# Gate and up steps of a quantized feed-forward layer: the step-size chain spread to one operation a step, and the second half's gate product moved from VectorE to GpSimd

## The chip, the cores and the metric

The kernel runs on one core of a Trainium2 chip. The metric is the device time of one execution in microseconds; lower is better. TensorE (PE in the profile) multiplies matrices into PSUM, VectorE (DVE) and ScalarE (ACT) do elementwise work and read PSUM, GpSimd (POOL) does elementwise work on SBUF tensors, and the SyncE queue (SP) issues the DMAs. The engines run side by side and are held in order by semaphores.

## The reference, cut to what matters

Two layers follow one another. The change lies where the second layer's feed-forward block and the first part of its state-space mixer are computed together, both from the normalized x:

```python
# feed-forward block: int4 weights with one scale per group of 128 inputs
Wg, Wu, Wd = dequant(gate_q, gate_s), dequant(up_q, up_s), dequant(down_q, down_s)
inner = silu(x @ Wg.T) * (x @ Wu.T)          # 1792 channels = 14 tiles of 128
g = silu(inner @ Wd.T)
# mixer: the step size of each of 128 heads and its running sum in chunks of 128 tokens
dt = softplus(h @ w_dt.T + dt_bias)          # = max(v, 0) + log(1 + exp(-|v|))
A_cs = cumsum(-exp(A_log) * dt)              # inside each chunk
```

1024 tokens stand as two halves (n = 0, 1) of 512 columns; channels are on the 128 partitions.

## The kernel before, in words

`layer1_inputs` computes `inner` in KI = 14 steps, one tile m of 128 channels a step. A step has both halves, n = 0 and then n = 1. For each half there are four groups k of 128 inputs, and for each of them a gate part and an up part: TensorE multiplies the unscaled integer weights with the tokens (`pe_group`, two passes each, L1075 and L1076) into one of four PSUM banks. The scales come in on the way out: ScalarE copies groups 0 and 1 with their scale into two sums (`act_group`, L1128), VectorE adds groups 2 and 3 to them (`dve_groups`, L1280, four operations a half), GpSimd adds the two sums (`add_sums`, L1574, two operations a half), ScalarE takes the silu of the gate part (`act_silu`, L1137), and the product of gate and up is `inner` (`dve_inner`, L1292, on VectorE for both halves). For the first half `inner` is split at once into a high and a low part for TensorE (`act_in` L1154, `dve_in_lo` L1269) and multiplied with the down weights of the step before; the down weights are scaled by VectorE (`dve_scale_down`, L1297) and split by ScalarE (`act_down`, L1143) and GpSimd (`rest_down`, L1579). GpSimd also turns the next tile's integer weights to floats (`whole_gate_up`, L1568). For the second half `inner` stays in the SBUF tensor `inner1` until all 14 steps are over; then 14 down steps (i = 14 to 27) multiply it.

Into the same steps the step-size chain is laid: `act_size` (step 1), `act_exps` (end of step 1), `act_plus_one` (step 2), `dve_rest` (steps 2 and 3), `act_logs` (end of step 3), `dve_dt` (two operations in each of steps 4 and 5), `dve_sums` (one operation and four scans in each of steps 6 and 7). The running sums `acs` are stored to DRAM by SP in step 10.

Each engine runs its instructions in the order in which they are written. On VectorE a step m is: four `dve_groups` of half 0; the product of step m - 1, half 1; `dve_scale_down`; the chain's part; the product of step m, half 0; four `dve_groups` of half 1; `dve_in_lo`. On GpSimd it is: two `add_sums` of step m - 1, half 1; `whole_gate_up`; two `add_sums` of step m, half 0; `rest_down`. Tiles are named by their memory: `sum_a` of odd steps lies in m_group, of even steps in f_sum_a and m_wdt; `sum_b` is g_stage; `inner1` is f_inner.

Of the kernel before, what the change touches and what calls it, by code (L numbers as in the profile page):

```python
# [9 lines left out]
ALU = mybir.AluOpType  # L10
# [915 lines left out]
def layer1_inputs(nc, a, xn, mv, x1_stored, ident, ones, h_hi, h_lo, xn_hi, xn_lo, std, normw, gu_s, group_dram,  # L926
# [9 lines left out]
    with ExitStack() as ctx:  # L936
# [50 lines left out]
        def gated(m):  # L987
            return inner1[:, (4 if m < 6 else 12) + m % 2, :]

# [61 lines left out]
        def half_at(m, n): return 2 * m + n  # L1051
# [126 lines left out]

        def act_exps(act):
            for n in range(NB):  # L1180
                act.wait_ge(act_chain, n + 1)
                nc.scalar.activation(e[:, n, :], rest[:, n, :], ACT.Exp, scale=-1.0).then_inc(act_chain, 1)
            nc.scalar.activation(aexp[:], alog[:], ACT.Exp).then_inc(aexp_ready, 1)
# [5 lines left out]

        def act_logs(act):  # L1190
            for n in range(NB):
                act.wait_ge(rest_ready, n + 1)
                nc.scalar.activation(u1[:, n, :], u1[:, n, :], ACT.Ln).then_inc(ln_ready, 1)

# [21 lines left out]

        def dve_dt(link, n):

            dve, c = nc.vector, slice(n * SEQ, (n + 1) * SEQ)
            dve.wait_ge(rest_ready, n + 1)  # L1220
            link(dve.scalar_tensor_tensor(rest[:, n, :], v[:, n, :], 0.0, rest[:, n, :], ALU.max, ALU.subtract))
            dve.wait_ge(ln_ready, n + 1)
            dve.tensor_tensor(dt[:, c], rest[:, n, :], u1[:, n, :], ALU.add).then_inc(dt_ready, 1)

        def dve_sums(link, n):

            dve, c = nc.vector, slice(n * SEQ, (n + 1) * SEQ)
            step = e[:, n, :]
            dve.wait_ge(dt_ready, n + 1)
            dve.wait_ge(aexp_ready, 1)  # L1230
            link(dve.tensor_scalar(step, dt[:, c], aexp[:, 0:1], -1.0, ALU.mult, ALU.mult))
            dve.wait_ge(gu_f_ready, 1)
            for t in range(TB):
                at = slice((n * TB + t) * P, (n * TB + t + 1) * P)
                dve.tensor_tensor_scan(acs[:, at], ones[:], step[:, t * P:(t + 1) * P], 0.0, ALU.mult,
                                       ALU.add).then_inc(acs_ready, 1)
# [45 lines left out]

        def dve_inner(dve, m, n):
            dve.wait_ge(silu_ready[n], m + 1)
            dve.wait_ge(sum_ready, 2 * half_at(m, n) + 2)
            if n == 0 and m >= 2:
                dve.wait_ge(in_lo_ready, m - 1)
            if n == 0 and m < 2:
                dve.wait_ge(h_lo_ready[1], m + 1)
            if n == 1 and m in (4, 5, 12, 13):  # L1290
                dve.wait_ge(in_lo_ready, m + 1)
            nc.vector.tensor_tensor(gated(m) if n == 0 else inner1[:, m, :], sum_a(m, n, 0), sum_a(m, n, 1),  # L1292
                                    ALU.mult).then_inc(inner_ready[n], 1)

# [23 lines left out]
        def _(sp):  # L1318
# [17 lines left out]
            for m in range(KI):  # L1336
                if m >= 2:
                    load_gate_up(m)
                load_down(m)
                if m == KI - 4:  # L1340
                    sp.wait_ge(acs_ready, NT)
                    sp.dma_start(acs_dram, acs[:]).then_inc(stored, 16)
# [72 lines left out]
        def _(act):  # L1415
# [21 lines left out]
            for m in range(KI):  # L1437
                if m:
                    act_group(act, m, 0, 0)
                    act_group(act, m, 0, 1)  # L1440
                    act_silu(act, m - 1, 1)
                if m == 1:
# [18 lines left out]
                if m == 1:  # L1461
                    act_exps(act)
                if m == 3:
                    act_logs(act)
            for i in range(KI, 2 * KI):
# [33 lines left out]
        def _(dve):  # L1499
# [31 lines left out]
            for m in range(KI):  # L1531
                if m:
                    dve_groups(dve, m, 0)
                    dve_inner(dve, m - 1, 1)
                dve_scale_down(dve, m + 1)
                if m in (2, 3):
                    dve_rest(m - 2)
                if m in (4, 5):
                    dve_dt(link, m - 4)
                if m in (6, 7):  # L1540
                    dve_sums(link, m - 6)
                dve_inner(dve, m, 0)
                if m < KI - 1:
                    dve_groups(dve, m, 1)
                    dve_in_lo(dve, m)
# [3 lines left out]
            for i in range(KI, 2 * KI):  # L1549
                if i == KI:  # L1550
                    dve_in_lo(dve, i)
                if i + 1 < 2 * KI:
                    dve_scale_down(dve, i + 1)
                    dve_in_lo(dve, i + 1)
                if i == KI + 2:
                    dve_inner(dve, KI - 1, 1)
                if i in (TURN_AT - 1, TURN_AT):
# [5 lines left out]
        def _(pool):  # L1563
# [33 lines left out]
            for m in range(KI):  # L1597
                if m:
                    add_sums(m - 1, 1)
                    if m + 1 < KI:  # L1600
                        whole_gate_up(m + 1)
                add_sums(m, 0)
                rest_down(m)
            for i in range(KI, 2 * KI):
                rest_down(i)
                if i == KI:
                    add_sums(KI - 1, 1)
                if W_AT < i <= W_AT + 4:
                    c, half = divmod(i - W_AT - 1, 2)
# [1269 lines left out]
```

## Time and profile before

| | |
|---|---|
| time, median of 3 runs | 1969.28 us (1967.21 to 1970.44) |
| the profiled execution's own time | 1965.4 us |
| its span, first to last instruction | 1963.6 us |
| PE busy | 1925.8 us, 98% |
| DVE busy | 1559.5 us, 79% |
| ACT busy | 1551.9 us, 79% |
| POOL busy | 1384.2 us, 70% |
| granted TensorE clock, mean | 0.999 |

The span is what the instructions cover; the execution's own time is 1.8 us more. The 14 steps lie between about 203 and 360 us of the span, the 14 down steps behind them up to about 408 us. Matmuls are pipelined: the record of one lasts 0.39 us, but the next starts 0.23 us after it, so a stretch in which PE is never idle can still hold fewer matmuls than it could. What counts is how many of them it starts.

### The profile page before, as it was taken

Reading aid. Unit: us, or ns where it says so; the run is one execution under the profiler, and the core shown is the slowest. Engines: PE = TensorE matmul, PEld = TensorE weight load, DVE = VectorE, ACT = ScalarE, POOL = GpSimd, SP = SyncE. Lnnn points to the kernel's source line nnn. Section 1 sums busy time; section 2 is a strip of 40 time slices with the busy share of each in tenths; the row PEclk is TensorE's granted clock in tenths of the full one; section 3 lists DMA queues with packets and bytes.
Section 4 is the critical chain, followed back from the end, with each engine's and each line's share of the span. In section 5 each row is a group of like instructions: output and inputs, shape, how many; then the busy total and the mean of one; then the engine's idle time right before and its main releaser. Section 6 shows DMA issues by size and latency. Waiting matters only on the chain.

```text
span 1963.6 us, 33121 instructions
## 1 busy us (share of the span) xinstructions
PE 1925.8 (98%) x10846; PEld 1562.4 (80%) x10846; DVE 1559.5 (79%) x2865; ACT 1551.9 (79%) x3105; POOL 1384.2 (70%) x976
## 2 busy tenths in 40 slices
PE   7999989999999999999999999999999999999998
PEld 6574767778888888888888888888888888888876
DVE  7787899967777777787777777777777878787878
ACT  5364866658898989897979797978888888888886
POOL 5644668546777777777777676777677777777787
PEclk9999999999999999999999999999999999999999
DMA  5615323554343333334333343434343434343333
GB/s 207 197 63 146 104 86 103 160 178 130 111 120 121 109 124 106 124 106 129 103 127 117 112 127 103 135 100 138 104 129 104 132 101 129 111 156 120 112 116 124
DMA packets 114475, 241.76 MB, mean 123 GB/s; under 512 B 23681, under 2 KB 24706, under 8 KB 113794
## 3 DMA queue, kind: packets, MB, share of 16 engines
q1 hardware_dynamic: 110466, 227.06, 36.4%
q0 software_dynamic: 3840, 12.59, 2.2%
q8 instruction: 89, 1.46, 0.3%
q14 instruction: 80, 0.66, 0.1%
HBM read 226.75 MB, written 12.85 MB: 122 GB/s over the span
## 4 chain that ended last, share of the span: by engine, by line
PE 76%; DVE 2%; ACT 1%; issue 1%; DVEq 0%; ACTq 0%
PE ps L75 19%; PE ps L77 19%; PE ps L76 19%; PE ps L2086 6%; PE ps L2050 4%; PE ps L2094 4%; PE ps L2042 3%; PE ps L2026 1%; PE ps L2034 0%; PE ps L2076 0%; DVE s_y_lo L2471 0%; DVE s_cv L2379 0%; ACT s_lm L2169 0%; DVE s_end_g L2635 0%; ACT s_scale L2184 0%
## 5 line engine op out<-in xcount | busy, mean ns | idle before, releaser
L2646 POOL TENSOR_TENSOR w_lo<-w_raw,w_hi 128x1024 fp32r<-128x1024 f32 x142 | 337.7, 2387 | 217.9 <-ACT w_hi L2152 217.9
L75 PE MATMUL ps<-h_hi,w_hi 128*128 128x512 f32 x1168 | 470.2, 403 | 4.0 <-POOL w_hi L865 1.6
L76 PE MATMUL ps<-h_lo,w_hi 128*128 128x512 f32 x1168 | 456.3, 391 | 0.0
L77 PE MATMUL ps<-h_hi,w_lo 128*128 128x512 f32 x1152 | 451.5, 392 | 0.0
L2379 DVE SCALAR_TENSOR_TENSOR s_cv<-ps,s_par,s_cv 128x511 f32<-128x511 f32 (+2 forms) x480 | 358.8, 748 | 113.5 <-ACT s_cv L2194 102.7
L2663 POOL TENSOR_TENSOR s_lm<-s_lm,s_cbt 128x512 f32<-128x512 f32 x256 | 327.6, 1301 | 122.2 <-ACT s_lm L2176 121.8
L2169 ACT ACTIVATE s_lm<-s_rows,s_steps 128x128 f32<-128x128 f32 x1024 | 318.6, 390 | 34.8 <-PE ps L2086 34.8
L75 PEld LDWEIGHTS ps<-h_hi,w_hi 128*128 128x128 f32 x1168 | 219.7, 188 | 53.4 <-DVE s_hid L2387 7.6
L76 PEld LDWEIGHTS ps<-h_lo,w_hi 128*128 128x128 f32 x1168 | 220.0, 188 | 42.1 <-issue 0.2
L77 PEld LDWEIGHTS ps<-h_hi,w_lo 128*128 128x128 f32 x1152 | 216.2, 188 | 46.9
L75 PE MATMUL ps<-s_wo_hi,s_y_hi 128*128 128x512 f32 x512 | 209.1, 408 | 1.7 <-DVE s_y_lo L2471 1.6
L2668 POOL TENSOR_TENSOR s_y_lo<-s_hid,s_y_hi 128x512 fp32r<-128x512 f32 x120 | 155.3, 1294 | 70.5 <-ACT s_hid L2228 70.5
L77 PE MATMUL ps<-s_wo_hi,s_y_lo 128*128 128x512 f32 x512 | 200.8, 392 | 0.0
L76 PE MATMUL ps<-s_wo_lo,s_y_hi 128*128 128x512 f32 x512 | 199.7, 390 | 0.0
L2200 ACT ACTIVATE ps<-s_cv 128x512 f32<-128x512 f32 x160 | 95.9, 599 | 102.4 <-DVE s_cv L2379 102.2
L2673 POOL TENSOR_TENSOR s_wo_lo<-s_wo_raw,s_wo_hi 128x512 fp32r<-128x512 f32 x128 | 166.1, 1297 | 0.0
L2152 ACT ACTIVATE w_hi<-w_raw 128x1024 fp32r<-128x1024 f32 x142 | 149.1, 1050 | 2.6 <-DMA w_raw<-in_w_in 1.4
L2176 ACT ACTIVATE s_lm<-s_lm 128x512 f32<-128x512 f32 x256 | 146.0, 620 | 0.0
L2214 ACT ACTIVATE s_y_hi<-s_hid,s_par 128x512 fp32r<-128x512 f32 x128 | 92.0, 718 | 61.9 <-DVE s_hid L2466 61.6
L2392 DVE SCALAR_TENSOR_TENSOR s_gate<-s_tg,ps 128x512 f32<-128x512 f32 x128 | 87.4, 683 | 67.2 <-ACT s_tg L2207 67.1
L2387 DVE SCALAR_TENSOR_TENSOR s_hid<-ps,s_cv 128x512 f32<-128x512 f32 x128 | 87.8, 686 | 65.1 <-ACT ps L2200 65.0
L2184 ACT ACTIVATE s_scale<-s_rows 64x384 f32<-64x384 f32 x256 | 132.9, 519 | 4.2
(323 smaller groups left out, 4233.8 us busy)
## 6 DMA issues: line engine op xcount, KB each, us to landing
w_raw<-in_w_in SPq DMA_DIRECT2D x144, 512.0 KB, 3.6
s_rows<-acs_dram SPq DMA_DIRECT2D x256, 256.0 KB, 3.6
s_wo_raw<-in_w_out SPq DMA_DIRECT2D x128, 256.0 KB, 3.2
w_raw<-in_gu_q SPq DMA_DIRECT2D x14, 512.0 KB, 3.6
f_d_q<-in_d_q SPq DMA_DIRECT2D x28, 256.0 KB, 2.6
f_d_w<-in_d_s SPq DMA_DIRECT2D x28, 256.0 KB, 3.4
table<-shifted SPq DMA_DIRECT2D x16, 256.0 KB, 2.9
xs<-in_x SPq DMA_DIRECT2D x8, 256.0 KB, 5.5
```

Source lines behind the costliest of these rows:

```text
L75: nc.tensor.matmul(dst, l_hi, r_hi, start=start, stop=False)
L76: nc.tensor.matmul(dst, l_hi, r_lo, start=False, stop=False)
L77: return nc.tensor.matmul(dst, l_lo, r_hi, start=False, stop=stop)
L2152: nc.scalar.activation(w_hi[:, slot, :], w_raw[:, slot, :], ACT.Copy).then_inc(w_hi_ready, 1)
L2169: ins = nc.scalar.activation(lm[:, h % 4, c], rows[:, h % 4, c], ACT.Relu, bias=steps[:, v.b, 2, i, h:h + 1], scale=-1.0)
L2176: nc.scalar.activation(lm[:, h % 4, :], lm[:, h % 4, :], ACT.Exp, scale=-1.0).then_inc(exp_ready, 1)
L2184: nc.scalar.activation(scale[e * HP:(e + 1) * HP, k % 2, :], rows[e * HP:(e + 1) * HP, h % 4, P:], ACT.Exp).then_inc(scale_ready, 1)
L2379: nc.vector.scalar_tensor_tensor(dst, src[:, 0:SEQ - d], par[:, v.b, 4 * j + 3 - d:4 * j + 4 - d], dst, ALU.mult, ALU.add).then_inc(conv_c ...
L2646: nc.gpsimd.tensor_tensor(w_lo[:, slot, :], w_raw[:, slot, :], w_hi[:, slot, :].bitcast(F32), ALU.subtract).then_inc(w_lo_ready, 1)
L2663: nc.gpsimd.tensor_tensor(lm[:, h % 4, :], lm[:, h % 4, :], cbt[:, v.b].rearrange("p c i -> p (c i)"), ALU.mult).then_inc(m_ready, 1)
L2668: nc.gpsimd.tensor_tensor(y_lo[:, k % 2, :], gated(un, k), y_hi[:, k % 2, :].bitcast(F32), ALU.subtract).then_inc(y_lo_ready, 1)
L2673: nc.gpsimd.tensor_tensor(wo_lo[:, k % 2, :], wo_raw[:, k % 2, :], wo_hi[:, k % 2, :].bitcast(F32), ALU.subtract).then_inc(wo_lo_ready, 1)
```

## The change

- `dve_inner` stays for the first half only. The second half's product is a new `pool_inner` on GpSimd. In step m GpSimd does the product of step m - 1 behind the two `add_sums` of half 0 and in front of `rest_down`; the last one comes behind `rest_down` of down step 16.
- The step-size chain gets one operation a step on VectorE: `dve_rest` in steps 2 and 3 as before, `dve_above` in 4 and 5, `dve_dt` in 6 and 7, `dve_step` in 8 and 9, the four scans of `dve_sums` in 10 and 11. The product with the rate is written to `u1` (rows 10 and 11 of `inner1`) and no longer to `e`.
- On ScalarE the exponentials and the logarithms of the two halves are no longer done together: the first half's stay where they were, the second half's (and the exponential of A_log) move into the next step, behind the copies of half 0 and in front of the silu.
- SP stores `acs` in step 12 and no longer in step 10. `gated` uses rows 6 and 7 of `inner1` in steps 6 and 7.

```diff
--- before.py
+++ after.py
@@ -985,7 +985,7 @@
             return xn_slots[lo][:, (i - KI - 1) % (NB * KD), :]
 
         def gated(m):
-            return inner1[:, (4 if m < 6 else 12) + m % 2, :]
+            return inner1[:, (4 if m < 6 else 6 if m < 8 else 12) + m % 2, :]
 
 
         h = inner1[:, 0:2, :]
@@ -1176,10 +1176,11 @@
                 act.wait_ge(v_ready, n + 1)
                 nc.scalar.activation(rest[:, n, :], v[:, n, :], ACT.Abs).then_inc(act_chain, 1)
 
-        def act_exps(act):
-            for n in range(NB):
-                act.wait_ge(act_chain, n + 1)
-                nc.scalar.activation(e[:, n, :], rest[:, n, :], ACT.Exp, scale=-1.0).then_inc(act_chain, 1)
+        def act_exp(act, n):
+            act.wait_ge(act_chain, n + 1)
+            nc.scalar.activation(e[:, n, :], rest[:, n, :], ACT.Exp, scale=-1.0).then_inc(act_chain, 1)
+
+        def act_rate(act):
             nc.scalar.activation(aexp[:], alog[:], ACT.Exp).then_inc(aexp_ready, 1)
 
         def act_plus_one(act):
@@ -1187,10 +1188,9 @@
                 act.wait_ge(act_chain, NB + n + 1)
                 nc.scalar.activation(u1[:, n, :], e[:, n, :], ACT.Identity, bias=ones[:, 0:1]).then_inc(u1_ready, 1)
 
-        def act_logs(act):
-            for n in range(NB):
-                act.wait_ge(rest_ready, n + 1)
-                nc.scalar.activation(u1[:, n, :], u1[:, n, :], ACT.Ln).then_inc(ln_ready, 1)
+        def act_log(act, n):
+            act.wait_ge(rest_ready, n + 1)
+            nc.scalar.activation(u1[:, n, :], u1[:, n, :], ACT.Ln).then_inc(ln_ready, 1)
 
         def act_decay_tile(act, t):
             act.wait_ge(acs_ready, t + 1)
@@ -1214,21 +1214,26 @@
             nc.vector.scalar_tensor_tensor(rest[:, n, :], u1[:, n, :], -1.0, e[:, n, :], ALU.add,
                                            ALU.subtract).then_inc(rest_ready, 1)
 
-        def dve_dt(link, n):
-
-            dve, c = nc.vector, slice(n * SEQ, (n + 1) * SEQ)
+        def dve_above(link, n):
+            dve = nc.vector
             dve.wait_ge(rest_ready, n + 1)
             link(dve.scalar_tensor_tensor(rest[:, n, :], v[:, n, :], 0.0, rest[:, n, :], ALU.max, ALU.subtract))
+
+        def dve_dt(n):
+
+            dve, c = nc.vector, slice(n * SEQ, (n + 1) * SEQ)
             dve.wait_ge(ln_ready, n + 1)
             dve.tensor_tensor(dt[:, c], rest[:, n, :], u1[:, n, :], ALU.add).then_inc(dt_ready, 1)
 
-        def dve_sums(link, n):
-
+        def dve_step(link, n):
             dve, c = nc.vector, slice(n * SEQ, (n + 1) * SEQ)
-            step = e[:, n, :]
             dve.wait_ge(dt_ready, n + 1)
             dve.wait_ge(aexp_ready, 1)
-            link(dve.tensor_scalar(step, dt[:, c], aexp[:, 0:1], -1.0, ALU.mult, ALU.mult))
+            link(dve.tensor_scalar(u1[:, n, :], dt[:, c], aexp[:, 0:1], -1.0, ALU.mult, ALU.mult))
+
+        def dve_sums(n):
+
+            dve, step = nc.vector, u1[:, n, :]
             dve.wait_ge(gu_f_ready, 1)
             for t in range(TB):
                 at = slice((n * TB + t) * P, (n * TB + t + 1) * P)
@@ -1280,17 +1285,26 @@
                     nc.vector.scalar_tensor_tensor(dst, ps[:, 2 * (k % 2) + part, :], gu_s[:, m, part, k:k + 1], dst,
                                                    ALU.mult, ALU.add).then_inc(group_added, 1)
 
-        def dve_inner(dve, m, n):
-            dve.wait_ge(silu_ready[n], m + 1)
-            dve.wait_ge(sum_ready, 2 * half_at(m, n) + 2)
-            if n == 0 and m >= 2:
+        def dve_inner(dve, m):
+            dve.wait_ge(silu_ready[0], m + 1)
+            dve.wait_ge(sum_ready, 2 * half_at(m, 0) + 2)
+            if m >= 2:
                 dve.wait_ge(in_lo_ready, m - 1)
-            if n == 0 and m < 2:
+            else:
                 dve.wait_ge(h_lo_ready[1], m + 1)
-            if n == 1 and m in (4, 5, 12, 13):
-                dve.wait_ge(in_lo_ready, m + 1)
-            nc.vector.tensor_tensor(gated(m) if n == 0 else inner1[:, m, :], sum_a(m, n, 0), sum_a(m, n, 1),
-                                    ALU.mult).then_inc(inner_ready[n], 1)
+            nc.vector.tensor_tensor(gated(m), sum_a(m, 0, 0), sum_a(m, 0, 1), ALU.mult).then_inc(inner_ready[0], 1)
+
+        def pool_inner(pool, m):
+            pool.wait_ge(silu_ready[1], m + 1)
+            pool.wait_ge(sum_ready, 2 * half_at(m, 1) + 2)
+            if m < 6:
+                pool.wait_ge(h_hi_ready, TB)
+                pool.wait_ge(h_lo_ready[1], 2)
+            if m in (4, 5, 6, 7, 12, 13):
+                pool.wait_ge(in_lo_ready, m + 1)
+            if m in (10, 11):
+                pool.wait_ge(acs_ready, (m - 9) * TB)
+            nc.gpsimd.tensor_tensor(inner1[:, m, :], sum_a(m, 1, 0), sum_a(m, 1, 1), ALU.mult).then_inc(inner_ready[1], 1)
 
         def dve_scale_down(dve, i):
             dve.wait_ge(d_loaded[i % 3], 32 * (i // 3 + 1))
@@ -1337,7 +1351,7 @@
                 if m >= 2:
                     load_gate_up(m)
                 load_down(m)
-                if m == KI - 4:
+                if m == KI - 2:
                     sp.wait_ge(acs_ready, NT)
                     sp.dma_start(acs_dram, acs[:]).then_inc(stored, 16)
             for i in range(KI, 2 * KI):
@@ -1438,6 +1452,11 @@
                 if m:
                     act_group(act, m, 0, 0)
                     act_group(act, m, 0, 1)
+                    if m == 2:
+                        act_exp(act, 1)
+                        act_rate(act)
+                    if m == 4:
+                        act_log(act, 1)
                     act_silu(act, m - 1, 1)
                 if m == 1:
                     act_size(act)
@@ -1459,9 +1478,9 @@
                 if m == 0:
                     act_biased(act)
                 if m == 1:
-                    act_exps(act)
+                    act_exp(act, 0)
                 if m == 3:
-                    act_logs(act)
+                    act_log(act, 0)
             for i in range(KI, 2 * KI):
                 act_down(act, i)
                 if i == KI:
@@ -1531,15 +1550,18 @@
             for m in range(KI):
                 if m:
                     dve_groups(dve, m, 0)
-                    dve_inner(dve, m - 1, 1)
                 dve_scale_down(dve, m + 1)
                 if m in (2, 3):
                     dve_rest(m - 2)
                 if m in (4, 5):
-                    dve_dt(link, m - 4)
+                    dve_above(link, m - 4)
                 if m in (6, 7):
-                    dve_sums(link, m - 6)
-                dve_inner(dve, m, 0)
+                    dve_dt(m - 6)
+                if m in (8, 9):
+                    dve_step(link, m - 8)
+                if m in (10, 11):
+                    dve_sums(m - 10)
+                dve_inner(dve, m)
                 if m < KI - 1:
                     dve_groups(dve, m, 1)
                     dve_in_lo(dve, m)
@@ -1552,8 +1574,6 @@
                 if i + 1 < 2 * KI:
                     dve_scale_down(dve, i + 1)
                     dve_in_lo(dve, i + 1)
-                if i == KI + 2:
-                    dve_inner(dve, KI - 1, 1)
                 if i in (TURN_AT - 1, TURN_AT):
                     dve_decay(i - TURN_AT + 1)
                 if i in (TURN_AT + 1, TURN_AT + 2):
@@ -1600,11 +1620,15 @@
                     if m + 1 < KI:
                         whole_gate_up(m + 1)
                 add_sums(m, 0)
+                if m:
+                    pool_inner(pool, m - 1)
                 rest_down(m)
             for i in range(KI, 2 * KI):
                 rest_down(i)
                 if i == KI:
                     add_sums(KI - 1, 1)
+                if i == KI + 2:
+                    pool_inner(pool, KI - 1)
                 if W_AT < i <= W_AT + 4:
                     c, half = divmod(i - W_AT - 1, 2)
                     cols = slice(half * D, (half + 1) * D)
```

## Rows read from the trace of the kernel before

**Rows 1.** The page: the span.

```profile
span 1963.6 us, 33121 instructions
```

**Rows 2.** Windows, one step: length; busy (count) of PE, PEld, DVE, ACT, POOL; clock, DMA.

```profile
311.40:322.00 10.60, 10.60 (x46) 8.01 (x45) 10.60 (x14) 7.21 (x13) 8.18 (x7) 1.00 0.31 103
```

**Rows 3.** PE's waits, 205 to 405 us: total, times, longest.

```profile
PE ps L1075 <- DVE m_group L1280: 2.7, 3, 1.4
PE ps L1075 <- ACT f_sum_a L1128: 1.7, 2, 0.9
```

**Rows 4.** DVE timeline, plain step: start, duration, engine, line, operation, out<-in, [idle before].

```profile
320.69 1.38 DVE L1292 TENSOR_TENSOR f_inner<-m_group 128x512 f32<-128x512 f32 x1
321.99 1.78 DVE L1297 TENSOR_TENSOR f_d_w<-f_d_q,f_d_w 128x512 f32<-128x512 int32 x1
323.69 0.68 DVE L1292 TENSOR_TENSOR f_inner<-f_sum_a 128x512 f32<-128x512 f32 x1
324.29 0.74 DVE L1280 SCALAR_TENSOR_TENSOR m_wdt<-ps,gu_s,m_wdt 128x512 f32<-128x512 f32 x1
...
326.93 1.79 DVE L1269 TENSOR_TENSOR f_in_lo<-f_inner,f_in_hi 128x512 fp32r<-128x512 f32 x1
...
331.29 1.39 DVE L1292 TENSOR_TENSOR f_inner<-m_wdt,f_sum_a 128x512 f32<-128x512 f32 x1
```

**Rows 5.** POOL timeline, adds of half 0 in two steps, and what follows the second.

```profile
298.88 3.51 POOL L1574 TENSOR_TENSOR f_sum_a<-f_sum_a,g_stage 128x512 f32<-128x512 f32 x2
...
320.23 2.99 POOL L1574 TENSOR_TENSOR f_sum_a<-f_sum_a,g_stage 128x512 f32<-128x512 f32 x2
325.63 1.29 POOL L1579 TENSOR_TENSOR f_d_lo<-f_d_w,f_d_hi 128x512 fp32r<-128x512 f32 x1 [2.41 <-ACT f_d_hi L1143]
```

**Rows 6.** DVE timeline, the step whose adds start at 298.88.

```profile
298.86 0.68 DVE L1292 TENSOR_TENSOR f_inner<-m_group 128x512 f32<-128x512 f32 x1
...
302.48 0.69 DVE L1292 TENSOR_TENSOR f_inner<-f_sum_a 128x512 f32<-128x512 f32 x1 [1.24 <-issue]
```

**Rows 7.** DVE timeline: middle stretch of step 1, of step 7 (scans), of step 13.

```profile
215.88 1.35 DVE L1292 TENSOR_TENSOR f_inner<-m_wdt,f_sum_a 128x512 f32<-128x512 f32 x1
...
219.46 1.39 DVE L1280 SCALAR_TENSOR_TENSOR m_group<-ps,gu_s,m_group 128x512 f32<-128x512 f32 x2
...
286.49 0.68 DVE L1292 TENSOR_TENSOR f_inner<-m_wdt,f_sum_a 128x512 f32<-128x512 f32 x1
...
288.79 1.51 DVE L1231 TENSOR_SCALAR f_inner<-m_dt,m_aexp 128x512 f32<-128x512 f32 x1
290.33 1.37 DVE L1235 TENSOR_TENSOR_SCAN m_acs<-ones,f_inner 128x128 f32<-128x128 f32 x4
...
292.21 1.40 DVE L1280 SCALAR_TENSOR_TENSOR m_group<-ps,gu_s,m_group 128x512 f32<-128x512 f32 x2
...
352.75 1.34 DVE L1292 TENSOR_TENSOR f_inner<-m_wdt,f_sum_a 128x512 f32<-128x512 f32 x1
...
356.31 1.40 DVE L1280 SCALAR_TENSOR_TENSOR m_group<-ps,gu_s,m_group 128x512 f32<-128x512 f32 x2
```

**Rows 8.** POOL timeline, two operations that a VectorE operation runs into.

```profile
282.42 1.88 POOL L1574 TENSOR_TENSOR m_wdt<-m_wdt,g_stage 128x512 f32<-128x512 f32 x1
...
374.60 1.30 POOL L1579 TENSOR_TENSOR f_d_lo<-f_d_w,f_d_hi 128x512 fp32r<-128x512 f32 x1 [1.29 <-ACT f_d_hi L1143]
```

**Rows 9.** DVE timeline, the operations that start just behind those of rows 8.

```profile
282.47 0.68 DVE L1269 TENSOR_TENSOR f_in_lo<-f_inner,f_in_hi 128x512 fp32r<-128x512 f32 x1
...
374.72 1.73 DVE L1297 TENSOR_TENSOR f_d_w<-f_d_q,f_d_w 128x512 f32<-128x512 int32 x1 [0.26 <-DMA f_d_w<-in_d_s]
```

**Rows 10.** ACT timeline, exponentials and logarithms of both halves.

```profile
222.04 1.15 ACT L1182 ACTIVATE f_inner<-f_inner 128x512 f32<-128x512 f32 x2
...
245.35 1.15 ACT L1193 ACTIVATE f_inner<-f_inner 128x512 f32<-128x512 f32 x2
```

**Rows 11.** DMA issues, the store of acs: issues, size, us to landing.

```profile
acs_dram<-m_acs SPq DMA_DIRECT2D x1, 512.0 KB, 4.5
```

## The prediction

> **What bounds the kernel now.** I read the page's span first [rows 1], then the windows over the steps, PE's waits, and last the timelines of VectorE and GpSimd side by side, because the change moves nothing on TensorE. In the windows a step without chain work takes 10.60 us and PE is busy all of it, but it starts only 46 matmuls there [rows 2], one per 0.230 us. A step has 44 (32 of the groups, 12 of the down weights), so TensorE alone would need 10.1 to 10.2 us. The 12 steps from the product that opens VectorE's middle stretch in step 1 (215.88) to the same one in step 13 (352.75) take 136.87 us [rows 7], 11.4 us each. So some 1.2 us a step is TensorE held back, and its waits name VectorE's group additions and, at two places of up to 0.9 us, ScalarE's group copies [rows 3]. VectorE is busy for all 10.60 us of the plain step [rows 2]: these steps run at VectorE's pace, and PE follows.
>
> I cut VectorE's step in two. The **middle stretch** M runs from T, the start of the operation behind the four group additions of half 0, to G, the first group addition of half 1. In the plain step T = 320.69, G = 324.29, M = 3.60 us, for three operations that need 0.60 us each [rows 4]. The **rest** R runs from G to the next T: 7.00 us here (324.29 to 331.29), where L1269 takes 1.79 us [rows 4], and 6.65 us where it takes 0.68 (292.21 to 298.86) [rows 6, 7].
>
> Why three operations of 0.6 us take 3.6 is seen with GpSimd's timeline beside it. The two adds run from 320.23 to 323.22 [rows 5]. L1292 at 320.69 takes 1.38 us and L1297 at 321.99 takes 1.78 us; L1292 at 323.69, when GpSimd idles, takes 0.68 [rows 4]. The two engines take turns, one whole instruction each: 1.24 us for a GpSimd add, 0.5 us for the VectorE operation (1.24 + 0.5 + 1.24 = 2.99), and the next VectorE operation starts 0.47 us behind the GpSimd one that let it in. A VectorE operation that already waits is let in before GpSimd's next. The Trainium skill says the same (SBUF — State Buffer, Who interferes with whom): a VectorE instruction with two SBUF inputs and a GpSimd instruction that reads SBUF exclude each other, and "Issue order, not op shape, decides who blocks." Operations that read PSUM (L1280) are not slowed: 0.74 us beside running adds.
>
> **The change, part by part.** *The product of the second half leaves VectorE.* That takes one turn of 0.5 to 0.6 us out of M. It doesn't shorten M by that, since the product of half 0 needs both adds done: in the step of rows 6, VectorE already sat idle 1.24 us for them.
>
> *It comes back on GpSimd right behind the second add.* That is the costly place. Its inputs have long been ready, so it starts as the second add ends (GpSimd instructions follow each other at -0.04 us), while VectorE's product of half 0 starts 0.09 us after that end (302.48 against 298.88 + 3.51 = 302.39) [rows 5, 6], thus some 0.13 us behind GpSimd's. The nearest rows: 0.05 us behind, VectorE won (0.68 us, the add grew to 1.88); 0.12 us behind, it lost (1.73 us, GpSimd's 1.30) [rows 8, 9]. So I let it lose. By the rule of issue order that the Trainium skill states there it would lose at every lag, and the sum would be the same; the win at 0.05 us speaks against so sharp a rule. The 2.41 us in which GpSimd idled in front of L1579 [rows 5] cover the new instruction on GpSimd's own account, and `rest_down` is not delayed (it starts 1.34 us after G either way); but what hides it on GpSimd blocks VectorE. Queued behind VectorE's waiting product are the four group additions of half 1, for which TensorE waits.
>
> The new M, with the adds starting 0.46 us ahead of T as in rows 4 (case B) or together with T as in rows 5 and 6 (case A):
> - plain, B: add ends at 0.78, scale 1.28, second add 2.52, GpSimd's product 3.76, G = 3.76 + 0.47 = 4.23 (before 3.60).
> - plain, A: scale first, 0.57; adds to 1.81 and 3.05; product 4.29; G = 4.76 (before 4.23: 302.48 + 0.60 - 298.86).
> - with one chain operation, B: 0.78, scale 1.28, add 2.52, chain 3.02, product 4.26, G = 4.73. A: 0.57, 1.81, chain 2.31, add 3.55, product 4.79, G = 5.26.
>
> A and B are tied to R: R = 7.00 goes with a following B, R = 6.65 with A, so their sums differ by under 0.2 us. I take the means: 4.5 plain, 5.0 with a chain operation.
>
> *The chain spread out.* Before, M was 3.58 in step 1 and 3.56 in step 13, and 5.72 in step 7 with L1231 (1.51 us, blocked, though it has one tensor input) and four scans (1.37 us) [rows 7]; over the 13 steps it sums to 56.4 us (first and last in rows 7; steps 2 and 3 hold 4.1 and 4.6, 4 to 7 hold 4.8 to 5.7). After: steps 1, 12 and 13 are plain, 3 x 4.5 = 13.5; steps 2 to 9 have one operation, 8 x 5.0 = 40.0; steps 10 and 11 have the scans. No row shows scans beside a GpSimd instruction. If they are never blocked, they fit in ahead of the second add's end and M is 4.5; if each takes its turn, two of GpSimd's fall between them and M is 5.95. They read two SBUF tensors as the products do, but for 0.32 us only; I take the middle, 2 x 5.2 = 10.4. Sum 63.9, that is **+7.5 us** (6.0 to 9.0 by the scans). The chain no longer stacks up in steps 4 to 7, but spread out it meets in each step a stretch that GpSimd has made longer.
>
> *ScalarE.* One exponential or logarithm (half of 1.15 us) [rows 10] moves from in front of half 0's copies to behind them, at the two places where PE waited up to 0.9 us for copies [rows 3]. With the small exponential this gives back 0.65 + 0.57 = **1.2 us**, at worst nothing. Table loads stay as many, since a silu follows each group of them anyway.
>
> *SP.* The store of acs now waits for the scans of step 11, and behind it in SP's queue stand the last gate and up weights (for the cast in step 12) and the down weights of step 13. The store landed after 4.5 us [rows 11]; from the scans' end to the cast there are about 2 us (rest of M) and 2.6 + 2.5 us (group additions, adds), 7 in all. I count nothing; if transfers share time, up to 1.5 us once.
>
> *The last product*, in the down steps, falls into GpSimd idle time and takes 0.6 us from a VectorE that waits for DMA there: nothing, within 0.3.
>
> **Sum.** +7.5 - 1.2 = +6.3 us; with the unknowns +4.8 to +10.5 (scans, ScalarE's gain lost, SP). TensorE bounds all that follows, so a delay here passes on whole. The profiled execution would go from 1965.4 to 1971.7 us. It lies 3.9 us under the median of the runs shown; on that median, 1969.28 + 6.3 = **1975.6 us**. A measurement of this kernel can tell about 0.2%, 3.9 us, from no change.
>
> **Rivals.**
> - *VectorE wins the tie* (faster). One mechanism: the semaphore reaches VectorE before GpSimd's product holds the ports. Then G comes 0.6 us behind the second add: M 3.2 to 3.75 plain, 3.6 to 4.25 with a chain operation, 3.9 with scans, sum 10.5 + 31.2 + 7.8 = 49.5, -6.9, with ScalarE's -1.2: 1961.2 us. It decides where the lag falls under some 0.05 us. For it: the win at 0.05. Against it: the loss at 0.12, and that with a chain operation GpSimd's product already waits when VectorE's arrives. 0.16.
> - *Mixed*: VectorE wins in plain steps and some others, and ScalarE's gain comes whole: about half of +7.5, so +2 to +3.9, 1971 to 1973. 0.17, with the case that the move has no effect at all.
> - *GpSimd becomes the bound*: six operations of 1.24, a cast of 1.0 and up to four turns of VectorE's 0.5 are 10.4 us, close to a step; with late weights from SP they push the adds behind T in most steps, 0.5 us more each: 1981 to 1986. 0.07.
> - *Forecast*: 0.60.
>
> The range takes in the forecast's bounds and the upper part of the mixed case: 1971.0 to 1980.0. Faster 0.16 (the first rival), same 0.20 (the mixed case and the lowest of the forecast's), slower 0.64.
>
> **What would show it.** Right: the product of half 0 takes 1.4 to 1.8 us in nearly all steps, M is 4.2 to 5.3 in steps 8, 9, 12 and 13, where it was 3.6 or 4.2, and under 5.3 in 4 to 7; L1579 starts 1.34 us after G as before; the gap at ScalarE's exponentials shrinks to under 0.5. Wrong: that product still takes 0.68 (then the first rival), steps shorter than 10.9 us, scans that stretch over 3 us, or GpSimd without idle time in front of L1579. What would upset the sum most is the order in which the two engines meet behind the second add, since 13 steps repeat it.

## The result

The changed kernel takes 1973.0 us (median of 8 runs, 1971.6 to 1975.4) where the kernel before took 1967.6 beside it (8 runs). The ratio is 1.0024, with a 95% interval of 1.0015 to 1.0033: by this ratio the change costs 4.7 us, between 3.0 and 6.5 (the two medians lie 5.4 us apart). The forecast was +6.3 us, that is 1975.6, with a range of 1971.0 to 1980.0. The profiled execution took 1971.8 us (before 1965.4), its span is 1970.0.

The page after has the same work on TensorE and ScalarE; the product's 14 instructions have gone from VectorE (2851, were 2865) to GpSimd (990, were 976). VectorE is no less busy for it: 1563.2 us, were 1559.5.

```profile
span 1970.0 us, 33127 instructions
## 1 busy us (share of the span) xinstructions
PE 1927.1 (98%) x10846; PEld 1559.8 (79%) x10846; DVE 1563.2 (79%) x2851; ACT 1551.7 (79%) x3105; POOL 1405.0 (71%) x990
```

PE's waits in the 14 steps and the down steps (total, times, longest) answer [rows 3]. VectorE's share has grown, from 2.7 to 4.4 us on m_group and from 1.7 to 3.0 on m_wdt; ScalarE's has shrunk from 1.7 to 0.7. The row of before that [rows 3] leaves out, and then the rows after:

```profile
PE ps L1075 <- DVE m_wdt L1280: 1.7, 2, 1.4
```

```profile
PE ps L1075 <- DVE m_group L1285: 4.4, 5, 1.3
PE ps L1075 <- DVE m_wdt L1285: 3.0, 4, 1.4
PE ps L75 <- DVE f_in_lo L1274: 1.5, 1, 1.5
PE ps L75 <- POOL f_d_lo L1599: 1.3, 2, 1.0
PE ps L1075 <- ACT f_sum_a L1128: 0.7, 2, 0.3
```

The cause is in the timelines. VectorE first, steps 7 (one chain operation), 11 (scans) and 13 (plain). Lines have new numbers: L1311 scales the down weights, L1295 is the product of half 0, L1285 the group additions.

```profile
286.96 1.40 DVE L1311 TENSOR_TENSOR f_d_w<-f_d_q,f_d_w 128x512 f32<-128x512 int32 x1
288.28 1.78 DVE L1226 TENSOR_TENSOR m_dt<-f_inner 128x512 f32<-128x512 f32 x1
289.98 1.78 DVE L1295 TENSOR_TENSOR f_inner<-m_group 128x512 f32<-128x512 f32 x1
291.68 1.40 DVE L1285 SCALAR_TENSOR_TENSOR m_group<-ps,gu_s,m_group 128x512 f32<-128x512 f32 x2
...
333.74 0.68 DVE L1311 TENSOR_TENSOR f_d_w<-f_d_q,f_d_w 128x512 f32<-128x512 int32 x1
334.33 4.58 DVE L1240 TENSOR_TENSOR_SCAN m_acs<-ones,f_inner 128x128 f32<-128x128 f32 x4
338.83 0.66 DVE L1295 TENSOR_TENSOR f_inner<-m_group 128x512 f32<-128x512 f32 x1
...
357.87 1.34 DVE L1311 TENSOR_TENSOR f_d_w<-f_d_q,f_d_w 128x512 f32<-128x512 int32 x1
360.45 1.71 DVE L1295 TENSOR_TENSOR f_inner<-m_group 128x512 f32<-128x512 f32 x1 [1.24 <-issue]
362.08 1.40 DVE L1285 SCALAR_TENSOR_TENSOR m_group<-ps,gu_s,m_group 128x512 f32<-128x512 f32 x2
```

GpSimd in steps 7 and 13: two adds (L1594), the product (L1307), the low part of the down weights (L1599).

```profile
286.51 3.00 POOL L1594 TENSOR_TENSOR m_group<-m_group,g_stage 128x512 f32<-128x512 f32 x2
289.47 1.74 POOL L1307 TENSOR_TENSOR f_inner<-m_wdt,f_sum_a 128x512 f32<-128x512 f32 x1
293.02 1.29 POOL L1599 TENSOR_TENSOR f_d_lo<-f_d_w,f_d_hi 128x512 fp32r<-128x512 f32 x1 [1.81 <-ACT f_d_hi L1143]
...
357.36 3.00 POOL L1594 TENSOR_TENSOR m_group<-m_group,g_stage 128x512 f32<-128x512 f32 x2 [0.90 <-DVE g_stage L1285]
360.32 1.29 POOL L1307 TENSOR_TENSOR f_inner<-m_wdt,f_sum_a 128x512 f32<-128x512 f32 x1
```

In step 13 GpSimd's product starts at 360.32 and VectorE's at 360.45, 0.13 us behind: VectorE's takes 1.71 us, where it took 0.68 before [rows 4]. In step 7 the chain operation (288.28) gets its turn between the second add and GpSimd's product, and then GpSimd's product gets its own in front of VectorE's at 289.98. In steps 10 and 11 the scans are the ones that wait (4.58 us in step 11), and VectorE's product behind them takes 0.66 us. The low part starts 1.34 us behind G, as before [rows 4, 5] (293.02 against 291.68): GpSimd's idle time hides the new instruction on GpSimd, and VectorE pays the price.

With T, G, M and R as in the prediction (M from T to G, R from G to the next T), the 13 steps from T of step 1 to G of step 13 make a sum that holds nothing but the changed stretch:

| us | before | after |
|---|---|---|
| M, steps 1 to 13 | 3.58 3.94 4.61 4.67 5.33 5.40 5.72 4.24 3.62 3.61 3.61 4.23 3.56 | 4.23 4.67 5.26 4.69 4.70 4.72 4.72 4.45 4.99 5.35 5.68 4.80 4.22 |
| sum of M | 56.1 | 62.5 |
| sum of R (12) | 84.3 | 83.0 |
| T of step 1 to G of step 13 | 140.4 | 145.5 |

That is +5.1 us. From G of step 13 to the mixer's first matmul it is 50.2 us, was 49.6. The other 0.7 us of the spans' 6.4 lie ahead of step 1, in code that is the same. T of step 1 stands anywhere from 215.9 to 219.6 us in these runs, so single spans can't be compared to a microsecond; this stretch can.

### The profile page after: what moved, and what is told of

Its sections match the earlier page's. It is cut to its first block, busy times and chain, and to the rows that moved or that the text cites. A ratio compares the mean times of both kernels' runs of the same rounds, so it can differ in the third digit from the quotient of the medians.

```text
span 1970.0 us, 33127 instructions
## 1 busy us (share of the span) xinstructions
PE 1927.1 (98%) x10846; PEld 1559.8 (79%) x10846; DVE 1563.2 (79%) x2851; ACT 1551.7 (79%) x3105; POOL 1405.0 (71%) x990
## 4 chain that ended last, share of the span: by engine, by line
PE 76%; DVE 2%; ACT 1%; issue 1%; DVEq 0%; ACTq 0%
PE ps L75 19%; PE ps L77 19%; PE ps L76 19%; PE ps L2110 6%; PE ps L2074 4%; PE ps L2118 4%; PE ps L2066 3%; PE ps L2050 1%; PE ps L2058 0%; PE ps L2100 0%; DVE s_y_lo L2495 0%; DVE s_cv L2403 0%; ACT s_lm L2193 0%; DVE s_end_g L2659 0%; ACT s_scale L2208 0%
```

## The experiments

Theory: two readers of SBUF take turns by order of start, and GpSimd's product takes its turn in front of VectorE's product of half 0. Rivals: the spread chain costs; GpSimd's load costs, whatever it does; the late store of acs costs. "Steps" in the results is T of step 1 to G of step 13, from the profile (before 140.4, after 145.5).

### One part alone: the product (e1)

```diff
 # the kernel before, with
-                    dve_inner(dve, m - 1, 1)
+                if m:
+                    pool_inner(pool, m - 1)      # behind add_sums(m, 0), in front of rest_down(m)
 # (cut: pool_inner's waits, fitted to the old chain, and the last product, as in the changed kernel)
```

> The kernel before with only the second half's product on GpSimd, behind the second add and in front of the low part of the down weights; chain, exponentials, logarithms and SP as before. Turn theory (VectorE's product of half 0 is shut out by GpSimd's product, 1.24 us each step): M about 4.5 in the seven plain steps, 5.0 in steps 2 and 3, 5.6 in 4 and 5, 6.4 in 6 and 7, sum 65.5 against 56.1, so +9.4 us, about 1977 where before is 1967.6. Rival (it is the chain spread over more steps that costs, the product alone saves VectorE 0.6 us a step): M 3.0 to 3.6 in plain steps, 1960 to 1967.

Measured: 1975.0 us, ratio 1.0035 (1.0022 to 1.0047), +6.9 us; steps 146.9. The theory's sign and place are right: M is 4.2 to 4.3 (once 4.8) in the plain steps. Its forecast was too high for the steps with two chain operations (5.6; measured 5.3) and with scans (6.4; measured 5.7 and 6.1). Step 5 shows why:

```profile
268.46 1.78 DVE L1221 SCALAR_TENSOR_TENSOR f_inner<-f_inner 128x512 f32<-128x512 f32 x1
270.28 1.67 DVE L1223 TENSOR_TENSOR m_dt<-f_inner 128x512 f32<-128x512 f32 x1
271.88 0.68 DVE L1290 TENSOR_TENSOR f_inner<-m_group 128x512 f32<-128x512 f32 x1
```

The product of half 0 (L1290) takes only 0.68 us here: GpSimd's product was already made while L1223 waited, so M is 5.3, as in step 5 before. Against before, M of steps 4 to 7 has grown by 0.62, 0.01, 0.32 and 0.35 us, that of the plain steps by 0.6 to 0.7 (only 0.05 in step 12). So the product alone costs the whole slowdown. In the steps it even costs 1.4 us more than the whole change; in the timed ratios the intervals overlap.

### One part alone: the chain (e2)

```diff
 # the changed kernel, with
+                    dve_second(dve, m - 1)       # VectorE, where the kernel before has it
-                    pool_inner(pool, m - 1)
 # (cut: dve_second has pool_inner's waits; the last product moves back too)
```

> The changed kernel with the second half's product back on VectorE, where it was; chain spread, exponentials and logarithms split, store of acs late. Turn theory: M 3.6 or 4.2 in plain steps, 4.1 or 4.6 with one chain operation, about 5 with scans, sum 56 to 57 as before; ScalarE's gaps give back 1.3 to 1.6 us: 1965 to 1967 where before is 1967.6. Rival (spreading the chain or the late store costs): 1970 to 1973, with R longer in steps 11 and 12.

Measured: 1967.1 us, ratio 0.9994 (0.9985 to 1.0003): no difference that can be told. Steps 139.6, 0.8 below before: M sums to 54.6 (1.5 less), R to 85.0 (0.7 more). The chain, the split exponentials and the late store don't cost; that rival falls. In the steps the two parts, +6.5 (e1) and -0.8, add up to +5.7 where both together measured +5.1: nearly additive.

One part of the expectation missed. R from step 1 to 2 and from step 3 to 4 is 8.11 and 8.01 us, as before, where ScalarE was to give back 1.3 to 1.6. PE's wait for ScalarE's copies did fall, from 1.7 to 0.6 us, but the second exponential now stands in front of the silu, and VectorE's product of half 1, which is still on VectorE here, waits for that silu in step 2 (0.77 us, where it was 0.16):

```profile
230.30 1.74 DVE L1307 TENSOR_TENSOR f_inner<-m_group 128x512 f32<-128x512 f32 x1 [0.77 <-ACT m_group L1137]
```

### GpSimd writes and doesn't read (e3)

```diff
-            nc.gpsimd.tensor_tensor(inner1[:, m, :], sum_a(m, 1, 0), sum_a(m, 1, 1), ALU.mult).then_inc(inner_ready[1], 1)
+            nc.gpsimd.memset(inner1[:, m, :], 0.0).then_inc(h_ready[0], 1)
+            pool.wait_ge(h_ready[0], m + 3)
+            nc.gpsimd.memset(inner1[:, m, :], 0.0).then_inc(inner_ready[1], 1)
```

> The changed kernel, where GpSimd writes zeros in the place of the second half's product (two memsets of 128x512, which read no SBUF tensor), so the second half of the feed-forward inner is left out; order, semaphores and GpSimd's place in the queue as after. Theory that two readers of SBUF shut each other out: VectorE's product of half 0 takes 0.68 us, M 3.2 to 3.8 in plain steps, some 8 to 12 us below after: 1961 to 1965. Rival (any instruction of GpSimd there, or its length in the queue, costs the same): 1972 to 1974.

Measured: 1962.1 us, ratio 0.9962 (0.9949 to 0.9975); steps 133.2, M sums to 50.5. This kernel leaves out the product of half 1 and writes zeros. The two memsets fill the product's place for 1.1 us. Step 9, GpSimd first and then VectorE:

```profile
308.45 0.52 POOL L1307 MEMSET f_inner<- 128x512 f32 x1
309.03 0.53 POOL L1309 MEMSET f_inner<- 128x512 f32 x1
```

```profile
308.71 0.69 DVE L1295 TENSOR_TENSOR f_inner<-m_group 128x512 f32<-128x512 f32 x1 [1.35 <-POOL m_group L1596]
309.31 1.40 DVE L1285 SCALAR_TENSOR_TENSOR m_group<-ps,gu_s,m_group 128x512 f32<-128x512 f32 x2
```

VectorE's product starts 0.26 us into the first memset and takes 0.69. So it is not the instruction's place in the queue, and not its length (1.1 us against the product's 1.24). The Trainium skill has this rule too (SBUF — State Buffer, Who interferes with whom): a VectorE instruction with two SBUF inputs contends with a GpSimd instruction that reads SBUF, not with one that only writes it; this trace agrees.

### The product yields (e4)

```diff
                 if m:
+                    pool.wait_ge(inner_ready[0], m + 1)
                     pool_inner(pool, m - 1)
```

> The changed kernel with one wait more: GpSimd's product of the second half starts only when VectorE's product of half 0 of the same step is done. Turn theory: VectorE's product takes 0.68 us, M 3.2 (adds early) or 3.7 (adds late) in plain steps, 3.6 or 4.2 with a chain operation, 4.4 to 5.0 with scans, sum about 50.5; GpSimd's product runs beside the group additions, which read PSUM, and ends about when the down weights' high part is ready, so L1579 still starts 1.3 to 1.5 us after G. 12 us below after: 1960 to 1963. Rival (GpSimd is the bound, a wait on it can only hurt): 1973 or more, L1579 1 us later after G.

Measured: 1962.2 us, ratio 0.9969 (0.9957 to 0.9981): one wait more and the kernel is 6.1 us faster than before, some 11 us faster than with the change as it stands. Steps 133.5, M sums to 51.3 (50.5 expected). VectorE and GpSimd in step 7:

```profile
282.86 0.68 DVE L1311 TENSOR_TENSOR f_d_w<-f_d_q,f_d_w 128x512 f32<-128x512 int32 x1
283.46 1.78 DVE L1226 TENSOR_TENSOR m_dt<-f_inner 128x512 f32<-128x512 f32 x1
286.48 0.69 DVE L1295 TENSOR_TENSOR f_inner<-m_group 128x512 f32<-128x512 f32 x1 [1.24 <-issue]
287.09 1.40 DVE L1285 SCALAR_TENSOR_TENSOR m_group<-ps,gu_s,m_group 128x512 f32<-128x512 f32 x2
```

```profile
282.88 3.51 POOL L1594 TENSOR_TENSOR m_group<-m_group,g_stage 128x512 f32<-128x512 f32 x2
287.25 1.30 POOL L1307 TENSOR_TENSOR f_inner<-m_wdt,f_sum_a 128x512 f32<-128x512 f32 x1 [0.86 <-DVE f_inner L1295]
288.51 1.29 POOL L1599 TENSOR_TENSOR f_d_lo<-f_d_w,f_d_hi 128x512 fp32r<-128x512 f32 x1
```

GpSimd waits 0.86 us and makes its product beside L1285, which reads PSUM and is not slowed. It is done 1.4 us behind G, about when the high part of the down weights is ready, so L1599 starts 1.42 us behind G instead of 1.34. Now the move does what it says: VectorE has one instruction less, and in PE's waits VectorE's two rows fall to 0.3 us each. Not all of the steps' 6.9 us arrive: from G of step 13 to the mixer it is 50.7 us, 1.1 more than before, and no run looked for the cause.

### The yielding product with the old chain (e5)

This is e1 with the wait of e4. 

> e1_product_only with the wait of e4: GpSimd's product starts only when VectorE's product of half 0 is done; chain, exponentials and logarithms as before. Turn theory (the gain is the turn saved in M, the spread chain adds only ScalarE's 1.3 to 1.6 us): M 3.2 to 3.7 in plain steps, 4.3 to 4.8 in steps 4 and 5, 5.0 to 5.5 in 6 and 7, steps 1 to 13 some 5.5 us shorter than before, 1962 to 1964 where before is 1968, 1 to 2 us above e4. Rival (with the product out of the way the spread chain is what gains): within 1 us of before.

Measured: 1964.5 us, ratio 0.9977 (0.9967 to 0.9987), steps 134.4. In the steps it is 0.9 us above the spread chain with the same wait (e4); the intervals of the two ratios overlap, so the times alone don't tell them apart. Nearly all of the gain is the yielding product's. The old chain's M is 4.3 to 5.0 in steps 4 to 7, and R behind steps 1 and 3, where ScalarE's exponentials and logarithms lie, is 7.87 and 7.78; split (e4) it is 7.27 and 7.25.

### A small delay, and two larger ones (e6, e9, e10)

The changed kernel, in which GpSimd waits for nothing on VectorE; a memset in front of its product only makes it later:

```diff
+                    nc.gpsimd.memset(spare[m], 0.0)             # e6: one column
                     pool_inner(pool, m - 1)
+            nc.gpsimd.memset(inner1[:, m, 0:128], 0.0).then_inc(h_ready[0], 1)   # e9; e10: 0:512
+            pool.wait_ge(h_ready[0], m + 3)
             nc.gpsimd.tensor_tensor(inner1[:, m, :], sum_a(m, 1, 0), sum_a(m, 1, 1), ALU.mult)...
```

> The changed kernel with a memset of one column (0.1 us) on GpSimd in front of its product, nothing else. GpSimd's product then starts just behind VectorE's product of half 0 in plain steps, and still before it where a chain operation is let in first. If the order of start decides to within 0.1 us: L1295 0.68 us and M 3.2 to 3.7 in steps 1, 12 and 13, unchanged at 4.7 in the steps with a chain operation, 3 us below after, 1969 to 1971. If it is not so sharp (or the engine that used the pair last keeps it): as after, 1972 to 1974.

Measured: 1973.8 us, ratio 1.0029 (1.0017 to 1.0040), steps 145.4: nothing gained, against the expectation. The memset of one column put the product back by 0.05 us only. Step 13, GpSimd and VectorE:

```profile
359.72 0.09 POOL L1626 MEMSET m_rrms<- 128x1 f32 x1
359.77 1.29 POOL L1309 TENSOR_TENSOR f_inner<-m_wdt,f_sum_a 128x512 f32<-128x512 f32 x1
```

```profile
359.86 1.75 DVE L1295 TENSOR_TENSOR f_inner<-m_group 128x512 f32<-128x512 f32 x1 [1.24 <-issue]
```

GpSimd is still 0.09 us ahead, and VectorE loses. The expectation mistook the memset's duration for the delay that it makes. Whether order of start decides was left open by it, so two longer delays followed.

> The changed kernel with a memset of 128 columns and a wait for it on GpSimd in front of its product (0.26 us), no wait for VectorE. GpSimd's product then starts 0.22 us behind the second add's end, VectorE's at 0.09 where it idles for the adds, at 0.48 where a chain operation is let in first. Order of start decides: L1295 0.68 us and M 3.2 to 3.7 in steps 1, 12, 13, and 4.2 in step 3; unchanged 4.7 in the steps where the chain operation waits for the second add. 3 to 5 us below after: 1968.5 to 1971. Rival (e6 has shown that the place in the queue decides and not the start): 1972 to 1974.

Measured: 1970.8 us, ratio 1.0014 (1.0005 to 1.0023), steps 141.8. Mostly as expected: M is 3.20, 3.24 and 3.21 in steps 1, 12 and 13, and 4.6 to 4.7 in the steps with a chain operation. Step 3 is one of these (4.72); 4.2 was expected there.

> As e9 with 512 columns (0.58 us): GpSimd's product starts 0.54 us behind the second add's end, so VectorE's is first in all steps, at 0.09 or at 0.48. Order of start: L1295 0.68 us in all steps, M as in e4, 1962 to 1965, though GpSimd does 0.5 us more in each step. Rival (a longer GpSimd costs): over 1967.

Measured: 1967.7 us, ratio 1.0003 (0.9994 to 1.0012), steps 140.0. Better again, but 3 us short of the expectation. Outside the steps with scans, VectorE's product was first only in steps 1, 3, 6, 7, 12 and 13. GpSimd in steps 5 and 6, then VectorE in steps 5, 6 and 8:

```profile
267.49 1.29 POOL L1309 TENSOR_TENSOR f_inner<-m_wdt,f_sum_a 128x512 f32<-128x512 f32 x1
...
279.32 1.78 POOL L1309 TENSOR_TENSOR f_inner<-m_group 128x512 f32<-128x512 f32 x1
```

```profile
267.53 1.80 DVE L1295 TENSOR_TENSOR f_inner<-m_group 128x512 f32<-128x512 f32 x1
...
279.25 0.68 DVE L1295 TENSOR_TENSOR f_inner<-f_sum_a 128x512 f32<-128x512 f32 x1
...
299.03 1.98 DVE L1232 TENSOR_SCALAR f_inner<-m_dt,m_aexp 128x512 f32<-128x512 f32 x1
```

In step 6 VectorE's product starts 0.07 us ahead and takes 0.68; in step 5, behind an operation whose end VectorE waits for (`link`), it starts 0.04 us behind and takes 1.80. So the order of start does decide, by less than 0.1 us. And in step 8 the chain's tensor_scalar, which took 1.52 us in the changed kernel, takes 1.98 (in step 9 too). It reads one tensor only, but it ends 0.3 us behind the memset (300.20 to 300.72) as if shut out by it, while L1226 beside the same memset stayed at 1.78. The down steps took back 1.7 us as well (51.3 us from G of step 13 to the mixer, 49.6 before). The four runs stand in a row: 1973.0, 1970.8, 1967.7 and 1962.2 with a wait instead of a delay, all with the same work on VectorE.

### Behind the low part, without a wait (e7)

```diff
-                if m:
-                    pool_inner(pool, m - 1)
                 rest_down(m)
+                if m:
+                    pool_inner(pool, m - 1)
```

> The changed kernel with GpSimd's product behind the low part of the down weights and not in front of it, no wait added. Turn theory: VectorE's product takes 0.68 us again, but GpSimd's now holds the pair when VectorE wants L1274, and half 1's adds start 1.24 us later: R 7.5 to 7.7 in nearly all steps, M 3.2 to 3.7 plain; between e4 and after, 1966 to 1972. Rival (only M matters): as e4, 1961 to 1963.

Measured: 1975.3 us, ratio 1.0039 (1.0023 to 1.0054), steps 145.8. Both expectations missed. VectorE's product takes 0.66 to 0.69 in every step, but R is not 7.5 to 7.7: it stays 6.65 to 7.0 (7.26 and 7.25 behind steps 1 and 3), and M is 4.8 to 5.6 with chain work. The delay is there and passes through GpSimd's queue: everything behind the product, half 1's adds, the cast and half 0's adds, starts 1.25 us later, and VectorE now waits for half 0's adds. ScalarE waits too, its silus for the late adds, and PE in turn for ScalarE's copies: 6.3 us in ten waits for g_stage, where the changed kernel has 0.2. GpSimd and VectorE in step 9:

```profile
310.06 1.29 POOL L1594 TENSOR_TENSOR f_sum_a<-f_sum_a,g_stage 128x512 f32<-128x512 f32 x1
311.31 1.50 POOL L1588 CAST w_hi<-w_raw 128x1024 fp32r<-128x1024 int32 x1
312.77 2.70 POOL L1594 TENSOR_TENSOR m_group<-m_group,g_stage 128x512 f32<-128x512 f32 x2
```

```profile
311.03 0.88 DVE L1311 TENSOR_TENSOR f_d_w<-f_d_q,f_d_w 128x512 f32<-128x512 int32 x1
...
315.67 0.69 DVE L1295 TENSOR_TENSOR f_inner<-m_group 128x512 f32<-128x512 f32 x1 [2.58 <-POOL m_group L1594]
```

From G to the start of the low part there is a slot of 1.3 us in which GpSimd has nothing to do and VectorE reads PSUM. In front of that slot the product blocks VectorE; behind it, GpSimd itself is late, the mechanism of the prediction's third rival.

### The store of acs later still (e8)

```diff
-                if m == KI - 2:
+                if i == KI:                      # in the down steps, behind load_down(i)
                     sp.wait_ge(acs_ready, NT)
                     sp.dma_start(acs_dram, acs[:]).then_inc(stored, 16)
```

> The changed kernel with SP's store of acs behind all loads of the 14 steps and the first of the down steps, so that no load waits for the scans. If the late store costs nothing, as the sum has it: as after, 1972 to 1974, M and R of steps 11 to 13 unchanged. Rival (loads that wait for the scans hold back the cast and the adds of step 12, where VectorE sat idle 2.49 us): up to 1.5 us faster than after, M of step 12 down from 4.80.

Measured: 1973.2 us, ratio 1.0025 (1.0015 to 1.0035), as the changed kernel's 1.0024. M of step 12 is 4.81, as in the changed kernel (4.80), and the steps are 145.3 us. The loads behind the store cost nothing that shows.

## Why the prediction was right

- **TensorE follows VectorE in these steps.** Right for the change: what it cost in the steps is in M, and the times of the runs follow their steps (133.2 to 146.9 us against 1962.1 to 1975.3) to within 3 us, of which the down steps of e5, e7, e9 and e10 have 1.5 to 2.0. In e7 VectorE and ScalarE both wait for GpSimd.
- **GpSimd's product starts 0.13 us ahead and VectorE loses.** Right to 0.01 us in steps 1, 3 and 13 (0.14, 0.12 and 0.13), where VectorE sits idle for the adds. In steps 4 to 7 VectorE's product arrives 0.5 to 0.6 us later than GpSimd's, behind its chain operation, as the prediction said against the first rival. The faster rival, VectorE winning the tie, would have needed a lag under some 0.05; e6 shows that at 0.09 it still loses.
- **The new M.** Plain: 4.23 and 4.76 forecast, 4.22 to 4.23 and 4.80 measured. With a chain operation: 4.73 and 5.26 forecast, 4.67 to 4.72 and 5.26 measured (the 4.67 of step 2 by another way: VectorE's product waits 0.70 us for ScalarE's silu and then takes 0.99). Too high was the forecast for steps 8 and 9, which measured 4.45 and 4.99: L1232, a tensor_scalar, takes 1.52 us there where L1226 takes 1.78, so its turn is some 0.26 us shorter than the 0.5 us I took. The scans were a guess between 4.5 and 5.95 and came out at 5.35 and 5.68: they do take turns (3.52 and 4.58 us for four, where 1.37 stands in [rows 7]). The prediction had named scans over 3 us as a sign that it is wrong; that sign came, and the sum held, because its upper bound for the scans already had them wait. The means of cases A and B were the other mis-sizing: six of the eight chain steps were case B, the shorter one. M sums to 62.5 against 63.9, and has grown by 6.4 us where 7.5 was forecast (M before was taken as 56.4 and is 56.1).
- **ScalarE gives back 1.2 us.** Right in size, but not by itself. R of steps 1 to 2 went from 8.11 to 7.25, of steps 3 to 4 from 8.01 to 7.25: 1.6 us, of which the rest of R took 0.3 back. With the old exponentials and the product moved (e1) the two are 7.87 and 7.75, so 0.5 of the 1.6 comes with the product and 1.1 with the split; e4 and e5 differ by 1.1 as well. The split alone (e2) leaves both as they were.
- **SP costs nothing.** Right, shown by e8.
- **The last product costs nothing within 0.3.** The down steps took 0.6 us longer after and 0.4 to 0.5 in e1, e6 and e8, which have the same order there, but 0.2 with the product on VectorE (e2). By that the term was 0.2 to 0.4 us too low; the cause stays open.
- **The sum.** +6.3 forecast, +5.1 in the steps and +5.7 with the down steps in the profile; the timed ratio says 4.7 (3.0 to 6.5), so +6.3 lies just inside. The excess is in M, 1.1 us too much, mostly the means of A and B and the tensor_scalar; the scans were too low by 0.6. Of the 2.6 us between 1975.6 and 1973.0, 1.6 are the median of before, 1969.28 when the forecast was made from three runs and 1967.64 with eight.

## What to carry to other kernels

An instruction moved to an engine with idle time is free only if it shares nothing there: look at what the old engine does in the moments in which the moved one will run. Where two engines shut each other out, place the movable instruction beside work that doesn't need the shared ports, and hold it there with a wait if its queue would let it go earlier: here one wait was worth 11 us. Where two instructions start within 0.1 us of each other, read their order from the timeline before you trust it.

## What the runs showed of the hardware

- Order of start decides sharply. Count, over steps 1 to 13 of all the traces, VectorE's products, scalings and splits that read two SBUF tensors and start within 0.2 us of a GpSimd instruction that reads SBUF. Those that started ahead or up to 0.02 us behind were never held back (67, none over 0.69 us); those 0.09 us or more behind always were (30, none under 1.38 us). From 0.03 to 0.07 us behind both happened (46 free, 75 held back), as in [rows 8, 9] and in e10. What decides there stays open.
- Short scans take part one by one: of four scans of 128 columns (0.39 to 0.40 us each when nothing holds them back, up to 1.52 when something does), two waited in step 10 and three in step 11, some 1.1 us each, by the sums of 3.52 and 4.58 us.
- A GpSimd memset leaves VectorE's tensor_tensor alone (0.69 us in e3), but a tensor_scalar from SBUF took longer beside one (1.98 us instead of 1.52 in e10). GpSimd's cast, with one SBUF input, waits its turn as well (1.50 us instead of 1.04 in e7).
- A GpSimd memset of one column shows 0.09 us and delays the next instruction by only 0.05; the next one starts 0.04 us ahead of the end that the profile shows.
